# A two-layer recurrent and attention kernel: the fourth pair's end moved into layer 1, its norm work put behind the finish, ScalarE's gelu ahead of the exponentials in every second sequence

## The reference

```python
xn = layernorm(x)
s  = recurrence(xn)                    # a complex decay along the sequence
g  = silu(moe32(xn) + shared(xn))      # 4 of 32 experts a token, and a gated shared one
x  = x + s * g
xn = layernorm(x)
s  = attention(xn)                     # softmax(q k^T) v inside each sequence
g  = silu(moe8(xn))                    # 2 of 8 experts a token, erf-gelu inside
x  = x + s * g
```

## Time and profile before

| | |
|---|---|
| median of 3 runs | 456.53 us |
| the profiled execution | 457.9 us, its span 456.0 us |
| TensorE busy | 381.0 us (84%) |
| TensorE's weight loads | 349.4 us (77%) |
| VectorE busy | 319.6 us (70%) |
| ScalarE busy | 257.6 us (56%) |
| GpSimd busy | 275.7 us (60%) |
| mean granted clock of TensorE | 0.94 |

### The profile page before, as it was taken

The page is one execution under the profiler, slowest core; times in us unless marked ns, Lnnn a source line. Parts: engine busy times, 40 slices in busy tenths (PEclk is TensorE's granted clock), DMA queues, the critical chain, the costliest instruction groups (busy, mean ns, idle before and its releaser), DMA issues. The chain is left out here.

```text
span 456.0 us, 8825 instructions
## 1 busy us (share of the span) xinstructions
PE 381.0 (84%) x2582; PEld 349.4 (77%) x2582; DVE 319.6 (70%) x1153; ACT 257.6 (56%) x505; POOL 275.7 (60%) x324
## 2 busy tenths in 40 slices
PE   0596986995089999997999897967998998889994
PEld 0584875884089999996999797856987977779983
DVE  6869588769137667766567648682699999995643
ACT  2233124421046767764776564537898886788882
POOL 5935777777777777763777777527777877100000
PEclk9999798898579999999999998978999999899998
DMA  7899995111257667537677563412222222000000
GB/s 183 257 376 310 291 390 180 53 54 46 90 176 213 215 224 219 201 127 240 196 227 217 171 207 101 139 54 56 64 60 70 67 58 65 24 14 25 12 24 23
DMA packets 45902, 65.16 MB, mean 143 GB/s; under 512 B 8586, under 2 KB 23331, under 8 KB 45859
## 3 DMA queue, kind: packets, MB, share of 16 engines
q1 hardware_dynamic: 37666, 47.83, 33.0%
q0 software_dynamic: 8192, 16.79, 12.6%
HBM read 28.93 MB, written 35.65 MB: 142 GB/s over the span
## 5 line engine op out<-in xcount | busy, mean ns | idle before, releaser
L550 POOL DMA_INDIRECT slot_rows<-xn_tok,slot_of x128 | 126.8, 991 | 49.7 <-issue 38.7
L564 POOL DMA_INDIRECT onehot<-expert_rows,slot_of x64 | 64.9, 1014 | 38.3 <-DMA expert_rows<-zeros 19.4
L564 POOL DMA_INDIRECT route_tmp<-expert_rows,slot_of x64 | 63.0, 985 | 19.5 <-issue 19.5
L1399 DVE TENSOR_TENSOR act<-sg,ps 128x384 f32<-128x384 f32 x48 | 26.5, 553 | 49.5 <-ACT sg L1007 48.6
L738 PE MATMUL ps<-w_dn,actT 96*128 x384 | 53.1, 283 | 5.1 <-ACT zeros L1016 5.1
L738 PEld LDWEIGHTS ps<-w_dn,actT 96*128 96x128 f32 x384 | 48.1, 197 | 5.9 <-issue 5.9
L1007 ACT ACTIVATE sg<-ps 128x384 f32<-128x384 f32 x48 | 23.5, 489 | 37.9 <-PE ps L747 37.2
L722 PE MATMUL ps<-ident,rows 128*128 128x128 f32 x192 | 29.9, 280 | 13.2 <-DMA rows<-slot_rows 11.6
L747 PE MATMUL ps<-w_gu,raw_fc 128*128 x192 | 37.8, 342 | 1.2 <-DVE act L1399 0.5
L1016 ACT COPY zeros<-ps 128x512 f32<-128x512 f32 x48 | 28.1, 585 | 17.7 <-PE ps L738 17.6
L824 PE MATMUL ps<-prT,rows 128*128 128x128 f32 x256 | 34.4, 291 | 3.4 <-DVE raw_fc L1548 3.4
(11 more groups left out here) (240 smaller groups left out, 899.1 us busy)
## 6 DMA issues: line engine op xcount, KB each, us to landing
slot_rows<-zeros SPq DMA_DIRECT2D x12, 1024.0 KB, 12.0
rows<-slot_rows SPq DMA_DIRECT2D x48, 256.0 KB
expert_rows<-zeros SPq DMA_DIRECT2D x48, 256.0 KB
x_tok<-in_L_attn_x_dram SPq DMA_DIRECT2D x8, 256.0 KB, 5.5
slot_rows<-xn_tok,slot_of POOLq DMA_INDIRECT x128, 2.4
out_dram<-raw_fc SPq DMA_DIRECT2D x16, 128.0 KB, 1.8
w_dn<-in_L_ffn_w_down_dram SPq DMA_DIRECT2D x1, 1536.0 KB, 17.1
onehot<-expert_rows,slot_of POOLq DMA_INDIRECT x64
```

The lines of the kernel that those rows point to most:

```text
L550: g.indirect_dma_start(out=slot_rows[r], out_offset=bass.IndirectOffsetOnAxis(ap=slot_of[:, n:n + 1], axis=0), in_=xn_tok[:, r * HT + t, : ...
L564: g.indirect_dma_start(out=gath[b % 4][:, j, :], out_offset=None, in_=expert_rows[r], in_offset=bass.IndirectOffsetOnAxis(ap=slot_of[:, n: ...
L1399: v.tensor_tensor(act[u][:].rearrange("p (a b) i -> p a b i", a=2), sg[u][:].rearrange("p (a b) i -> p a b i", a=2), ps[:, 1 + 2 * u:3 + 2 ...
```

## The change

Pair 3 gets its turn inside layer 1 (`NORM_AT` 2 in place of -1): the sum of experts of sequence 7, mix, statistics, reciprocal root and normalisation leave the end of layer 0, and silu there with them; they stand in turns 1 and 2. Its gates and pair 2's become batches of their own. The first projection and values of layer 1 go into the last group of layer 0 (`first_products`, `first_kept`), with the last down-projection in bank 0, so that it waits for no copy of bank 6. In VectorE's loop the gate product comes first, ahead of the reciprocal, and statistics, reciprocal root and sum of experts go behind the finish and the gates. ScalarE does gelu ahead of the exponentials in odd sequences, and TensorE makes the hidden rows of an odd sequence one turn earlier, ahead of the output. `expert_sum` and its tanh wait for the first step of the finish that reads the bank, in place of its end. Moved functions without another change are left out.

```diff
...
-NORM_AT = {-1: 3, 4: 4, 6: 5, 8: 6, 10: 7}
-BATCHES = ((0, 2), (2, 2), (4, 1), (5, 1), (6, 1), (7, 1))
+NORM_AT = {2: 3, 4: 4, 6: 5, 8: 6, 10: 7}
+BATCHES = ((0, 2), (2, 1), (3, 1), (4, 1), (5, 1), (6, 1), (7, 1))
...
-        if b >= 0 and turned(b + ahead) is not None:
+        if b > 0 and turned(b + ahead) is not None:
...
-    if b == -1:
-        return 0
-    for k, (first, count) in enumerate(BATCHES[1:], 1):
+    if b in (-1, 0):
+        return b + 1
+    for k, (first, count) in enumerate(BATCHES[2:], 2):
         if turned(b - 2) == first + count - 1:
             return k
...
+        def down_bank(n):
+
+            return 0 if n == N - 1 else 6
...
             def down(n, u, e, first=False):
                 pe.wait_ge(e_aTs, n + 1)
-                if not first:
+                if not first and n < N - 1:
                     pe.wait_ge(e_out, n)
                 for j in range(GT):
-                    mm = pe.matmul(ps[:, 6, j * P:(j + 1) * P], actT[u][:, j * P:(j + 1) * P],
+                    mm = pe.matmul(ps[:, down_bank(n), j * P:(j + 1) * P], actT[u][:, j * P:(j + 1) * P],
...
+            def first_products():
+
+                pe.wait_ge(biases, 2)
+                pe.wait_ge(c_lgs, FSEQ // 2 - 1)
+                pe.wait_ge(e_act, N - 1)
+                project(0)
+                values(0)
...
+                pe.matmul(ps[:, 6 if b else 1, 0:SEQ], w1T[:, 0:P], turned_rows(b), start=True, stop=True).then_inc(d_qk, 1)
...
+                if n == N - 1:
+                    turn = first_products
...
-            pe.wait_ge(e_out, N)
-            pe.wait_ge(c_lgs, FSEQ // 2 - 1)
 
             def expert_sum(b, u, first):
                 pe.wait_ge(d_hs, b + 1)
                 if not first:
-                    pe.wait_ge(d_fin, b)
+                    pe.wait_ge(d_moe_read, b)
...
-            project(0)
-            values(0)
+            pe.wait_ge(e_out, N - 1)
             scores(0)
+            pe.wait_ge(e_act, N)
+            hidden_of(0)
+            pe.wait_ge(e_out, N)
             for b in range(NSEQ):
                 u = b % 2
-                hidden_of(b)
+                if b and not u:
+                    hidden_of(b)
...
+                if not u:
+                    hidden_of(b + 1)
                 output(b, u)
...
-                a.copy(eo[slot], bank(6)).then_inc(e_out, 1)
+                a.copy(eo[slot], bank(down_bank(n))).then_inc(e_out, 1)
...
+                a.activation(key_of, ps[:, 6 if b else 1, 0:SEQ], ACT.Identity, bias=w1T[:, 2 * P + 1:2 * P + 2],
...
+            def first_kept():
+
+                sc.wait_ge(biases, 2)
+                shift_projected(0)
+                keep_values(0, 0)
+
+            def exponentials(b):
+                sc.wait_ge(d_nmx, b + 1)
+                for j in range(2):
+                    last = a.activation(pr[:, j, :], pr[:, j, :], ACT.Exp,
+                                        bias=nmx[:, j:j + 1], scale=-1.0, accum_out=den[:, j:j + 1])
+                last.then_inc(d_p, 1)
+                if b + 1 < NSEQ:
+                    shift_projected(b + 1)
+
+            def gelu(b, u):
+                sc.wait_ge(d_h, b + 1)
+
+                if b >= 2:
+                    sc.wait_ge(d_moe, b - 1)
+                a.activation(hg[u], ps[:, 4:6, :].rearrange("p a (b n) -> p (a b) n", b=2),
...
-                if step == 2:
+                if step == 2 and q < FSEQ // 2 - 1:
                     after = lambda: silu_f(q)
                 if step == 0 and q == FSEQ // 2 - 1:
                     after = lambda: tanh_gates(0)
+                if n == N - 1:
+                    turn = first_kept
+                    sc.wait_ge(sent[1], 16 * HT * TOP0)
                 if half_starts(n):
                     start_half(n)
                 stage_e(n, turn, after)
 
...
-            sc.wait_ge(sent[1], 16 * HT * TOP0)
...
-                    sc.wait_ge(d_fin, b)
+                    sc.wait_ge(d_moe_read, b)
...
-            shift_projected(0)
-            keep_values(0, 0)
...
+                if u:
+                    gelu(b, u)
+                    exponentials(b)
+                else:
+                    exponentials(b)
+                    gelu(b, u)
                 batch, place = batch_of(b)
...
                 if step == 1:
                     sum_experts(2 * q)
-                if step == 2 and n < N - 2:
-                    sum_experts(2 * q + 1)
-                if step == 3:
-                    mix(q, False)
-                    stats1(q)
-                if step == 4:
-                    rstd1()
+                if q < FSEQ // 2 - 1:
+                    if step == 2:
+                        sum_experts(2 * q + 1)
+                    if step == 3:
+                        mix(q, False)
+                        stats1(q)
+                    if step == 4:
+                        rstd1()
...
-                if step == 2 and n == N - 2:
-                    sum_experts(2 * q + 1)
-            rstd1()
-            norm1(FSEQ // 2 - 1)
...
             def finish(b, u, first, used):
 
                 dve.wait_ge(d_mth, b + 1)
-                link(v.scalar_tensor_tensor(out=mg[:].rearrange("p a d -> p (a d)"), in0=mth[:], scalar=1.0,
-                                            in1=bank(3, SEQ), op0=ALU.add, op1=ALU.mult))
+                if b:
+                    dve.wait_ge(d_fin, b)
+                v.scalar_tensor_tensor(out=mg[:].rearrange("p a d -> p (a d)"), in0=mth[:], scalar=1.0,
+                                       in1=bank(3, SEQ), op0=ALU.add, op1=ALU.mult).then_inc(d_moe_read, 1)
+                dve.wait_ge(d_moe_read, b + 1)
                 dve.wait_ge(d_os, b + 1)
                 link(v.tensor_tensor(mg[:], mg[:], o_sb[u][:], ALU.mult))
...
             for b in range(NSEQ):
                 u = b % 2
-                if turned(b) is not None:
-                    stats1(turned(b))
-                    rstd1(summed(b))
-                elif summed(b) is not None:
-                    sum_experts(summed(b))
+                gate_hidden(b, u)
                 dve.wait_ge(d_p, b + 1)
                 if b:
                     dve.wait_ge(d_os, b)
                 v.reciprocal(rden[:], den[:]).then_inc(d_rden, 1)
-                gate_hidden(b, u)
                 if b + 1 < NSEQ:
                     least(b + 1, 1 - u)
                 if b:
@@ -1586,7 +1612,11 @@
                 if gated(b) is not None:
                     top_gates(gated(b))
                 if turned(b) is not None:
+                    stats1(turned(b))
+                    rstd1(summed(b))
                     norm1(turned(b))
+                elif summed(b) is not None:
+                    sum_experts(summed(b))
                 if turned(b + 1) is not None:
                     mix(turned(b + 1), True)
             finish(NSEQ - 1, 1, False, NSEQ // 2 - 1)
...
```

More of the change, by code:

```diff
@@ L365, in build @@
         d_fin = sem("d_fin")
+        d_moe_read = sem("d_moe_read")
         stored = [sem(f"stored{u}") for u in range(2)]
@@ L797, in stage_e, with turned_rows, project, values @@
                     down(n, n % 2, ids(n * GT))
+            def turned_rows(b):
+                return xn_tok[:, b * 2:b * 2 + 2, :]
+            def project(b):
+                pe.wait_ge(c_xn_kept, b // 2 + 1)
+                if b:
+                    pe.wait_ge(d_nmx, b)
+                pe.matmul(ps[:, 6 if b else 1, 0:SEQ], w1T[:, 0:P], turned_rows(b), start=True, stop=True).then_inc(d_qk, 1)
+            def values(b):
+                if b:
+                    pe.wait_ge(d_vs, b)
+                for j in range(2):
+                    pe.matmul(ps[:, 7, j * VW:(j + 1) * VW], ones_bf[:], bv_rows[:], start=True, stop=False)
+                    mm = pe.matmul(ps[:, 7, j * VW:(j + 1) * VW], turned_rows(b)[:, j, :], w1T[:, P:P + VW],
+                                   start=False, stop=True)
+                mm.then_inc(d_v, 1)
             for n in range(N):
@@ L840, in _ @@
             pe.wait_ge(biases, 2)
-            def turned_rows(b):
-                return xn_tok[:, b * 2:b * 2 + 2, :]
-            def project(b):
-                pe.wait_ge(c_xn_kept, b // 2 + 1)
-                if b:
-                    pe.wait_ge(d_nmx, b)
-                pe.matmul(ps[:, 6, 0:SEQ], w1T[:, 0:P], turned_rows(b), start=True, stop=True).then_inc(d_qk, 1)
-            def values(b):
-                if b:
-                    pe.wait_ge(d_vs, b)
-                for j in range(2):
-                    pe.matmul(ps[:, 7, j * VW:(j + 1) * VW], ones_bf[:], bv_rows[:], start=True, stop=False)
-                    mm = pe.matmul(ps[:, 7, j * VW:(j + 1) * VW], turned_rows(b)[:, j, :], w1T[:, P:P + VW],
-                                   start=False, stop=True)
-                mm.then_inc(d_v, 1)
             def scores(b):
@@ L1065, in stage_e, with shift_projected, keep_values @@
                     after()
```

(20 more changed lines are left out.)

24 lines of the change are left out of this document (1 added, 23 removed).

## The result

The changed kernel takes **487.41 us** (median of 4 runs, 485.86 to 490.38) against 456.89 us before (4 runs); the ratio is 1.0657, 95% interval 1.0581 to 1.0734. The forecast was 476 us with a range of 463 to 486, so the direction and the place were right and the size was not. The profiled execution took 488.28 us, its span 486.5.

A forecast was written before the change was run, and what follows sets the result against it. VectorE bounds layer 1's pairs before; after, ScalarE's chain behind the late sum does. Gate product 11 at 432.9 plus a 42.8 tail gives span 475.7, 19.7 more; from the median 476 us, range 463 to 486.

The forecast's parts named there:

- The start: End of layer 0 to the first gate product: it would come at 305.5 in place of 313.34, 7.8 us gained.
- VectorE's bill: VectorE in layer 1: 96 us of work from gate product 1 to 11 without idle time, 20.13 a full pair.
- The late sum: Odd sequences: ScalarE's tanh waits until VectorE has made the sum of experts, 17.97 us after the even gate product.
- The rival that VectorE alone decides: Layer 1 pairs: the chain hides beside VectorE's work; 449 to 454 us, or 465 with half its cost; 16 in 100.
- the chain: ScalarE from tanh to the next even gate product: 6.81 us behind the late sum, making a pair 24.8 against 20.1.
- The step that failed: TensorE's logits, expert sum, turned gates and shares finish before the gates' copy at the higher clock; nothing charged.
- a rival with 2.5 us a pair and 486 us: TensorE's clock falls after idling near 5 us a pair: 2.5 a cycle, four cycles 10 more, 486; 12 in 100.
- the main forecast: In layer 1 pairs ScalarE's chain waits for VectorE's late sum: 476 us, own range 469 to 481; 68 in 100.
- The sum: Gate products 1 at 315.3, 2 at 327.8, 4 at 349.2, 10 at 423.5, 11 at 432.9; span 475.7.
- Tables and tail: 15 fewer loads free 19.2 us of ScalarE, none counted; the tail after gate product 11 stays 42.8 us.

The follow-up runs named there:

- run 1: Against the changed kernel, VectorE makes the odd sequence's sum of experts ahead of the gate product again; 458.46 us, ratio 1.0003.
- Run 4: Against the changed kernel, TensorE makes 5 or 11 unread products ahead of the gate logits in turns 4, 6, 8 and 10; 479.77 us, ratio 1.0483.
- run 3: Against the changed kernel, ScalarE makes exponentials ahead of gelu in every turn, with 32 table loads again; 493.85 us, ratio 1.0796.
- run 7: Against the changed kernel, odd sum of experts ahead of the gate product and exponentials ahead of gelu in every turn; 466.90 us, ratio 1.0147.
- run 8: Against the changed kernel, odd sum of experts ahead of the gate product and rows normalised by ScalarE; 462.14 us, ratio 1.0028.
- run 10: Against run 1, transposes, gate logits and copy of transposed rows moved later, rows still normalised on VectorE; 459.28 us, ratio 1.0006.
- run 9: Against run 8, transposes behind the next hidden rows, logits behind the expert sum, copy behind the weighing; 454.39 us, ratio 0.9918.

## Why the prediction came out short

**The start** was forecast with gate product 0 at 305.5 and came at 308.40. In the kernels with the same start it lay between 306.82 and 310.07, so some 5 of the forecast 7.8 us were gained. From the first exponentials (302.58) to gate product 0 it was 5.82 us, as charged; the part ahead of them was 2.9 us longer than forecast. The last output copy started at 299.23 in place of 297.8, and the exponentials' table, which the prediction loads beside the scores and the minimum at no cost, was loaded only behind the wait for the minimum, as the last thing ahead of the exponentials:

```profile
301.29 1.28 ACT L1107 ACT_TABLE_LOAD   x1 [1.47 <-DVE hs_h L1587]
```

**VectorE's bill** was right. The prediction counted 96 us of work from gate product 1 to 11 if nothing else held it up, of which 20.13 in a full pair; run 1 took 95.9 us (318.72 to 414.61) and 20.14. Before, the same stretch took 90.0 us, since the fourth pair's end lay ahead of it. That is where the change's gain goes even with the sum in time: 4.5 us earlier at gate product 0 in run 1, some 6 us more work on VectorE behind it, and run 1 is no faster than before.

**The late sum** was right, in its place and size. The odd tanh came 18.07 us after the even gate product (353.10 to 371.17; forecast 17.97), and run 1 shows that it alone makes the change slow. The rival that VectorE alone decides described run 1, not this kernel: with the sum behind the gates, nothing but the mix is left on VectorE to cover the chain.

**The step that failed** is the price of that chain on TensorE: "by the order they are done before the gates' copy, if TensorE keeps its higher clock, so I charge nothing for it here." It doesn't keep it. From tanh to gate product the chain took 9.14 us (371.17 to 380.31) in place of 6.81, because the expert sum at the lower clock ended behind ScalarE's gelu and the gates' copy then waited for TensorE. Run 4 measures it apart: at a granted clock of 1.00 the chain takes 6.55 us and the pair 24.44, close to the forecast 6.81 and 24.8, and the lower clock adds 2.68 a pair. The prediction had this as a rival with 2.5 us a pair and 486 us, at 12 in 100, and named the sign of it, even gate products 27 apart; they are. By the rows at hand it deserved more weight: a wait of 5 us for TensorE in each pair was part of the main forecast itself, and the trace of the kernel before has slowed expert sums behind far shorter waits. The earlier trace rows shows one of 2.86 us behind 0.58 us of idle time (three others behind the same 0.58 were not slowed), and the last expert sum of that trace ran at a granted clock of 0.55:

```profile
448.40 3.44 PE L824 MATMUL ps<-prT,rows 128*128 128x128 f32 x16 [1.03 <-DVE raw_fc L1548]
```

The Trainium skill, TensorE: Matmul & The Clock Gate, describes in its section on oscillation a loop that waits for a transfer in each step, so that each step starts at the lower clock, and advises to restructure the loop so that TensorE keeps the higher one. The trace agrees on the pattern, with 0.87 in three pairs out of three, though the wait here is for another engine.

**The sum** by terms, of the 10.8 us between the forecast span (475.7) and the profiled one (486.5): 3.1 at gate product 1 (318.37 against 315.3); nothing from 1 to 2; 0.9 from 2 to 4 (353.10 less 330.78, 22.3 against 21.4), where the expert sum was slowed in part; 7.1 in the three pairs to gate product 10 (81.45 against 74.4), which is the clock's 2.68 a pair less 0.3 by which the rest of a pair was shorter than forecast; and the tail 0.3 shorter than forecast. Either of the two misses alone would have left the time inside the stated range: without the 3.1 at the start it would be 484.3, without the 8.0 between gate products 2 and 10 479.4.

**Tables and tail.** The tail of 42.8 was left as it was and took 42.53. That two things cancel there was forecast, but not their size: with exponentials first the new order's tail takes 46.05 (run 3), so gelu first is worth 3.5 us there, and the rest of the new order costs 3.2 against the kernel before. Which part of it costs that, no run here tells; that the sum came out so close is luck. In the pairs of the changed kernel gelu first gave nothing (run 3); with the sum in time it gave 0.8 us a pair (run 7).

## What to carry to other kernels

When an order by hand is changed on one engine, look at what the other engines' lists have standing at that point: here ScalarE's tanh kept its place while the sum that it needs moved behind 5.3 us more of VectorE's work (gate product to finish, and the gates), and a chain that had lain beside VectorE's work came behind it. If a forecast contains a wait of some microseconds for TensorE in each step, price the work behind that wait at the lower clock as well, by the slowest such row in the trace. And where one engine sets the pace, move its work elsewhere only together with the places in the other queues that wait for that work: either half alone gave nothing here, both 0.8%.

## What was not expected of the hardware

- Some 22 unneeded matmul records a pair made the kernel faster: with them TensorE's granted clock stays at 1.00 instead of 0.87, and 2.68 us a pair come back, more than half as much as the wait itself (4.78 us) had been.
- The order of gelu with fifteen table loads less, 19.2 us of ScalarE, was worth nothing in the old order of VectorE (ratio 0.9992), and 6.6 us of the span in the new one with the sum in time.
- Single pairs of other kernels took 1.3 to 1.6 us longer at a granted clock of 0.92 (the second window of run 8; one pair in run 10, 383.01 to 404.49), where the pair ahead, in the same order, had 1.00. What sets this off was not settled.
- ScalarE needs 1.65 us for the normalisation of four tiles of 128x128, VectorE 1.12; once the queues behind were reordered (run 9), the slower engine was the better place, since it had the time.
